# Two groups of SBUF-to-SBUF transfers of the attention layers, issued from ScalarE's queue instead of SyncE's

## The chip, the cores and the metric

The kernel runs on one core of a Trainium2 chip. The time is the device time of one execution in microseconds (us). Five engines work from queues of their own: TensorE (PE: matmuls, with the weight loads shown apart as PEld), VectorE (DVE), ScalarE (ACT), GpSimd (POOL) and SyncE (SP), which computes nothing and issues DMA transfers. They meet through semaphores: an instruction may wait until a counter has reached a value, and counts one up when it is done; a transfer counts its semaphore up by 16 when it has landed.

## The reference, cut to what matters

A batch of 32 sequences of 256 tokens and 256 features goes through two cross-attention layers and two feed-forward layers:

```python
x = x + L0_xattn(layernorm(x), ctx, ctx)    # 16 heads of 16, LoRA projections
x = x + L0_ffn(layernorm(x))                # sqrt(real^2 + imag^2)
x = x + L1_xattn(layernorm(x), ctx, ctx)    # 16 heads of 16, rotary embedding
x = x + L1_ffn(layernorm(x))                # quantised, gelu

def attention(q, k, v):                     # per batch and head
    attn = softmax(q @ k.T / sqrt(16))
    return attn @ v                         # then the output projection Wo
```

The change concerns what stands between `attn @ v` and the output projection. The kernel computes exponentials that are not normalised, multiplies them with v extended by a column of ones, and so gets for each head 16 weighted sums and the sum of the exponentials, the denominator. The division comes afterwards.

## The kernel before, in words

Both attention layers are one function, `attention`, with `layer` 0 or 1 (L0 and L1 below). It is a software pipeline over the 32 batches: each engine runs `step(i)` with 16 slots k = 0 to 15. In slot k TensorE does two matmuls of the scores of batch i + 1 (`scores`, L480) and two of the transposed scores of batch i (`scores_T`, L498); VectorE reduces the first for the row maxima (L690) and ScalarE takes the exponential of the second (L590). Both PSUM banks (`s_bank`, `t_bank`) have two halves, used in turn, so `scores_T` of slot k waits until the exponential of slot k - 2 is done (L495, semaphore `act_p`).

All other work of a batch is hung into the slots by the table `PLACE`: `"dn": (-1, 8)` says that in step i, slot 8, the engine that has the operation does it for batch i - 1. Within a slot each engine follows the order of the code. The table is an order and not a clock: SyncE's step numbers run apart from those of the others, and only the semaphores hold them together. The operations that matter here, for batch n:

- `pe0`, `pe1` (ScalarE, L600): copy the sums of half h of the heads from PSUM (`eo`) to `osb`. `pe1` is in step n + 1, slot 1 in L0 and slot 0 in L1.
- `dn` (SyncE, L270 to L273): wait for both copies, then one transfer of the denominators from 4 partitions of `osb` into `den` (128 partitions of 32).
- `mg` (SyncE, L274 to L279): wait until `den` has landed, then four transfers, each moving 16 partitions of the second half of `osb` beside the sums of the first.
- `rd` (VectorE, L706) takes the reciprocal of `den`; `rs` and `rb` (SyncE, L283, L287) send it through memory and spread it over the partitions of `rb`; `ym` (GpSimd, L378) waits for `rb` and for the merge and multiplies; `yh` and `yl` split the product, and `o0`, `o1` (TensorE, L467) are the output projection of the batch.
- SyncE's other work of a batch: twelve transfers that stack the q and k parts (`st0`, `st1`, L258), two of the maxima (`ml0`, `ml1`, L263), the context, and in L1 two for the rotation.
- ScalarE's other work in the middle of a step: `ms0` (L595, a small copy that waits for VectorE's reduction of slot 7), `qe` and `ke` (L610, the copies of the projected q and k with bias, which wait for TensorE), and in L1 `hh` (L622). `qe` of L0 is in slot 10, `qe` of L1 in slot 6, `ms0` in slot 7 in both.
- TensorE's: `q0`, `q1`, `k0`, `k1` (L460), `v0`, `v1`, `o0`, `o1` (L467), `xT` (L522), `mT0`, `mT1` (L515) and the four `pv` groups (L566).

Of the kernel before, what the change touches and what calls it, by code (L numbers as in the profile page):

```python
# [15 lines left out]
H, HD = 16, 16  # L16
RANK = 16
DFF = 1024
P = 128
# [19 lines left out]
def after(eng, sem, value):  # L39

    if not (isinstance(value, int) and value <= 0):
        eng.wait_ge(sem, value)  # L42
# [12 lines left out]
class Core:  # L55
# [12 lines left out]
    def sems(self, prefix, names):  # L68
# [20 lines left out]
)  # L89
# [72 lines left out]
def attention(core, layer, sem, f_sem, tiles, w, x_res, stats, extent, consts, src, scratch):  # L162
# [14 lines left out]
    cT, xn, xT, hl, osb, yT, yhl, rb = tiles.cT, tiles.xn, tiles.xT, tiles.hl, tiles.osb, tiles.yT, tiles.yhl, tiles.rb  # L177
    negm, mhi, mT, less_high, den, rden = tiles.negm, tiles.mhi, tiles.mT, tiles.less_high, tiles.den, tiles.rden
# [19 lines left out]
    sem = dict(sem, **core.sems(f"L{layer}", "b_load w_load rstd ones_set bvx ones0 pe_bo bo whl_q whl_k whl_v whl_o"  # L198
                                + (" rot prod sum" if rope else " lora lora_w less v_set eo_set pick high_c"
                                   " x_load0 x_load1 x_load2 x_load3 x_load4 ident")))  # L200
# [3 lines left out]
    def on(n):  # L204
        return lo <= n < hi

    def due(op, i, k):

        ahead, slot = place[op]
        return [i + ahead] if slot == k and on(i + ahead) else []  # L210
# [36 lines left out]
    def sync_program(sp):  # L247
        def all_ones():
            sp.wait_ge(sem["ones_set"], 1)
            for buf in kst:  # L250
                for u in range(2):
                    sp.dma_start(buf[64 * u + ROWS:64 * u + ROWS + 2, :, :, :].bitcast(F32), ones).then_inc(sem["ones0"], 16)

        def stack(n, h):
            u = n % 2 ^ h
            for dst, parts in ((kst[n % 2], (0, 0, 1)), (qst[n % 2], (2, 3, 2))):
                for c, part in enumerate(parts):
                    sp.dma_start(dst[64 * u + c:64 * u + ROWS:3, :, :, :].bitcast(F32), hl[h::2, part, :, :].bitcast(F32)).then_inc(sem[f"stack{h}"], 16)  # L258

        def maxima(n, h):  # L260
            u = n % 2 ^ h
            sp.wait_ge(sem["dve_mT"], 2 * n + h + 1)
            sp.dma_start(qst[n % 2][64 * u + ROWS:64 * u + ROWS + 2, :, :, :].bitcast(F32), mT[h][:, :].bitcast(F32)).then_inc(sem[f"m_load{h}"], 16)  # L263

        def step(i):
            for k in range(16):
                for h in range(2):
                    for n in due(f"ml{h}", i, k):
                        maxima(n, h)
                for n in due("dn", i, k):  # L270
                    sp.wait_ge(sem["act_eo"], 2 * n + 2)
                    after(sp, sem["dve_rd"], n)
                    sp.dma_start(den[:, :], osb[n % 2][HD:P:32, :, :, :]).then_inc(sem["den_load"], 16)  # L273
                for n in due("mg", i, k):  # L274
                    sp.wait_ge(sem["den_load"], 16 * (n + 1))
                    after(sp, sem["merge"], 64 * n)
                    for g in range(4):
                        sp.dma_start(osb[n % 2][32 * g + HD:32 * (g + 1), 0, :, :],
                                     osb[n % 2][32 * g:32 * g + HD, 1, :, :]).then_inc(sem["merge"], 16)  # L279
                for n in due("rs", i, k):  # L280
                    sp.wait_ge(sem["dve_rd"], n + 1)
                    after(sp, sem["r_load"], 16 * n)
                    sp.dma_start(r_dram.rearrange("(p n) -> p n", p=P), rden[:, :]).then_inc(sem["r_store"], 16)  # L283
                for n in due("rb", i, k):
                    sp.wait_ge(sem["r_store"], 16 * (n + 1))
                    after(sp, sem["pool_y"], n)
                    sp.dma_start(rb[:, :, :], r_dram.rearrange("(h a n) -> h a n", h=8, a=1).to_broadcast([8, HD, KT * S])).then_inc(sem["r_load"], 16)  # L287
                for h in range(2):
                    for n in due(f"st{h}", i, k):
                        sp.wait_ge(sem["pool_low"], n + 1)  # L290
                        after(sp, sem["pe_t"], 16 * (n - 2) + 8 * h + 8)
                        after(sp, sem[f"stack{h}"], 96 * n)
                        if rope and n <= lo + 1:
                            sp.wait_ge(f_sem["pe_mm"], B)
                            sp.wait_ge(f_sem["dve_x"], B)
                        stack(n, h)
                        if n == lo and h == 0:
                            all_ones()
                for n in due("ctx", i, k):
                    if rope:  # L300
                        after(sp, sem["pe_v"], max(n - 1, lo))
                        after(sp, sem["pe_k"], max(n - 1, lo))
                        after(sp, sem["ctx_load"], 16 * n)
                        sp.dma_start(cT[n % 2][:, :, :, :].bitcast(F32), c_dram[n - lo]).then_inc(sem["ctx_load"], 16)
                    else:
                        after(sp, sem["pool_c"], n - 1)
                        after(sp, sem["ctx_load"], 16 * n)
                        sp.dma_start(ctx_in[n % 2], src["ctxT"][n - lo]).then_inc(sem["ctx_load"], 16)
                if not rope:
                    for n in due("cs", i, k):  # L310
                        sp.wait_ge(sem["pool_c"], n + 1)
                        sp.dma_start(c_dram[n - lo], cT[0][:, :, :, :].bitcast(F32)).then_inc(sem["c_store"], 16)
                else:
                    for n in due("rot", i, k):
                        sp.wait_ge(sem["act_k"], n + 1)
                        sp.wait_ge(sem["act_q"], n + 1)
                        after(sp, sem["sum"], n - lo)
                        for h in range(2):
                            sp.dma_start(kqr[64 * h:64 * (h + 1), :, :, :], kq[64 * (1 - h):64 * (2 - h), :, :, :]).then_inc(sem["rot"], 16)

        return step
# [260 lines left out]
    def scalar_program(act):  # L582
        def step(i):
            for k in range(16):
# [11 lines left out]
                for h in range(2):  # L596
                    for n in due(f"pe{h}", i, k):
                        act.wait_ge(sem["pe_pv"], 4 * n + 2 * h + 2)
                        after(act, sem["pool_y"], n - 1)
                        act.activation(osb[n % 2][:, h, :, :], eo[:, :, :], ACT.Copy).then_inc(sem["act_eo"], 1)  # L600
                for n in due("xTh", i, k):
                    act.wait_ge(sem["pe_xT"], n + 1)
                    after(act, sem["pe_q"], n)
                    act.activation(xT[:, 0, :, :], bank["xT"][:, :, :], ACT.Copy).then_inc(sem["act_xT"], 1)
# [905 lines left out]
```

## Time and profile before

| | |
|---|---|
| median of 3 runs | 1902.04 us (1901.72 to 1903.93) |
| profiled execution | 1900.1 us, its span from first to last instruction 1898.3 us |
| TensorE clock granted, mean | 0.921 of full speed |
| PE busy | 1634.1 us (86%) |
| DVE, ACT, POOL busy | 1323.1, 1231.2, 848.8 us |
| all transfers, issued by SyncE | 281.34 MB, mean 148 GB/s |

The stages in order of time: a start of about 100 us, L0 to about 640 us, the first feed-forward with the first batches' preparation for L1 to about 830 us, L1 to about 1520 us, and the second feed-forward. The page gives the busy time of each engine and, in 40 slices of the span, its share in tenths with the clock that TensorE was granted. Issuing a transfer does not count as busy time; it is shown under SPq.

### The profile page before, as it was taken

Reading aid. Unit: us, or ns where it says so; the run is one execution under the profiler, and the core shown is the slowest. Engines: PE = TensorE matmul, PEld = TensorE weight load, DVE = VectorE, ACT = ScalarE, POOL = GpSimd, SP = SyncE. Lnnn points to the kernel's source line nnn. Section 1 sums busy time; section 2 is a strip of 40 time slices with the busy share of each in tenths; the row PEclk is TensorE's granted clock in tenths of the full one; section 3 lists DMA queues with packets and bytes.
Section 4 is the critical chain, followed back from the end, with each engine's and each line's share of the span. In section 5 each row is a group of like instructions: output and inputs, shape, how many; then the busy total and the mean of one; then the engine's idle time right before and its main releaser. Section 6 shows DMA issues by size and latency. Waiting matters only on the chain. (4 is left out here: it accounts for less than half of the span.)

```text
span 1898.3 us, 38948 instructions
## 1 busy us (share of the span) xinstructions
PE 1634.1 (86%) x13992; PEld 1236.5 (65%) x13992; DVE 1323.1 (70%) x2567; ACT 1231.2 (65%) x2194; POOL 848.8 (45%) x670
## 2 busy tenths in 40 slices
PE   5699999999999889778988888988989838894987
PEld 4567777777776477566666666666666536663977
DVE  5767777777777778645666767677766457776976
ACT  1267777777777678636666666666666528885875
POOL 3235555555454231145665566656665122222432
PEclk9699999999999899959899999899998759997999
DMA  8366766766776310066666666676666115557785
GB/s 249 87 142 161 151 167 161 149 165 159 155 162 152 85 50 23 17 123 141 146 140 144 144 147 147 140 150 148 152 137 138 41 39 207 213 221 270 253 274 180
DMA packets 152485, 281.34 MB, mean 148 GB/s; under 512 B 39904, under 2 KB 66144, under 8 KB 144096
## 3 DMA queue, kind: packets, MB, share of 16 engines
q1 hardware_dynamic: 152304, 278.96, 57.6%
q8 instruction: 110, 1.80, 0.5%
q14 instruction: 71, 0.58, 0.1%
HBM read 89.99 MB, written 59.77 MB: 79 GB/s over the span
## 5 line engine op out<-in xcount | busy, mean ns | idle before, releaser
L690 DVE TENSOR_REDUCE L_negm<-L_s_bank 128x2 f32<-128x512 f32 x1024 | 661.6, 682 | 364.3 <-PE L_s_bank L480 363.3
L590 ACT ACTIVATE L_prob<-L_t_bank 128x512 f32<-128x512 f32 x1024 | 573.8, 597 | 316.3 <-PE L_t_bank L498 307.6
L480 PE MATMUL L_s_bank<-L_kst,L_qst 48*128 48x256 f32 x2048 | 441.1, 327 | 60.3 <-DVE L_negm L690 45.1
L498 PE MATMUL L_t_bank<-L_qst,L_kst 50*128 50x256 f32 x2048 | 434.3, 324 | 21.2 <-ACT L_prob L590 16.4
L480 PEld LDWEIGHTS L_s_bank<-L_kst,L_qst 48*128 48x128 f32 x2048 | 301.8, 195 | 214.8 <-DVE L_negm L690 118.6
L498 PEld LDWEIGHTS L_t_bank<-L_qst,L_kst 50*128 50x128 f32 x2048 | 298.4, 194 | 35.0 <-ACT L_prob L590 24.0
L566 PE MATMUL L_eo<-L_prob,L_vext 128*17 128x256 f32 x4096 | 271.8, 397 | 3.4 <-ACT L_prob L590 3.3
L409 POOL TENSOR_TENSOR L_hl<-L_kq,L_hl 128x1024 fp32r<-128x1024 f32 x64 | 152.1, 2376 | 64.5 <-ACT L_hl L622 61.8
L1280 PE MATMUL G_acc<-G_w_out,G_hhl 128*128 128x256 f32 x1024 | 132.9, 290 | 44.8 <-DVE G_hhl L1249 44.8
L566 PEld LDWEIGHTS L_eo<-L_prob,L_vext 128*17 128x17 f32 x4096 | 103.2, 100 | 101.3 <-issue 15.6
L1280 PEld LDWEIGHTS G_acc<-G_w_out,G_hhl 128*128 128x128 f32 x1024 | 127.4, 195 | 50.6 <-issue 27.5
L610 ACT ACTIVATE L_kq<-L_misc,L_bqk 128x256 f32<-128x256 f32 x256 | 107.4, 474 | 74.6 <-PE L_misc L460 55.6
L362 POOL TENSOR_TENSOR L_kqr<-L_kqr,L_cs 128x1024 f32<-128x1024 f32 x32 | 75.9, 2373 | 161.8 <-DMA L_kqr<-L_kq 161.8
L460 PE MATMUL L_misc<-L_xT,L_wq 128*128 128x256 f32 x768 | 140.5, 326 | 2.5 <-DVE L_xT L702 1.6
L1017 PE MATMUL G_hb<-G_xT,G_w_in 128*128 128x512 f32 x512 | 127.4, 402 | 11.9 <-DVE G_xT L1127 11.2
L378 POOL TENSOR_TENSOR L_yT<-L_osb,L_rb 128x512 f32<-128x512 f32 x64 | 82.3, 1286 | 120.4 <-DMA L_rb<-r_scratch 120.2
L460 PE MATMUL L_misc<-L_cT,L_wk 128*128 128x256 f32 x768 | 119.5, 312 | 11.9 <-POOL L_cT L392 4.9
L412 POOL TENSOR_TENSOR L_yhl<-L_yT,L_yhl 128x512 fp32r<-128x512 f32 x64 | 82.6, 1290 | 102.6 <-ACT L_yhl L626 102.2
L460 PEld LDWEIGHTS L_misc<-L_xT,L_wq 128*128 128x128 f32 x768 | 114.4, 217 | 17.3 <-issue 4.3
L460 PEld LDWEIGHTS L_misc<-L_cT,L_wk 128*128 128x128 f32 x768 | 111.6, 219 | 18.1 <-issue 13.3
L1017 PEld LDWEIGHTS G_hb<-G_xT,G_w_in 128*128 128x128 f32 x512 | 94.9, 190 | 38.0 <-ACT G_hid L1059 14.2
L467 PE MATMUL L_misc<-L_wv,L_cT 128*128 128x256 f32 x768 | 119.0, 299 | 0.0
(161 smaller groups left out, 2608.6 us busy)
## 6 DMA issues: line engine op xcount, KB each, us to landing
L_kst<-L_hl SPq DMA_DIRECT2D x384, 128.0 KB, 3.4
L_qst<-L_hl SPq DMA_DIRECT2D x384, 128.0 KB, 4.1
hidden_scratch<-G_hid SPq DMA_DIRECT2D x32, 1024.0 KB, 3.9
G_hid<-hidden_scratch SPq DMA_DIRECT2D x32, 1024.0 KB, 7.4
c_scratch<-L_cT SPq DMA_DIRECT2D x32, 512.0 KB, 4.9
L_rb<-r_scratch SPq DMA_DIRECT2D x64, 256.0 KB
L_cT<-c_scratch SPq DMA_DIRECT2D x32, 512.0 KB, 3.6
L_kqr<-L_kq SPq DMA_DIRECT2D x64, 256.0 KB, 4.3
```

The costliest lines, as they stand in the source:

```text
L409: pool.tensor_tensor(KQ_LOW, kq[:, :, :, :], KQ_HIGH.bitcast(F32), ALU.subtract).then_inc(sem["pool_low"], 1)
L412: pool.tensor_tensor(yhl[:, 1, :, :], yT[:, :, :], yhl[:, 0, :, :].bitcast(F32), ALU.subtract).then_inc(sem["pool_yl"], 1)
L460: mm = pe.matmul(bank[x][:, f, :], whl[x][:, cw, k, P * f:P * (f + 1)], act[:, ca, k, :], start=j == 0, stop=j == 5)
L467: mm = pe.matmul(bank[x][:, t, :], act[:, ca, k, P * t:P * (t + 1)], whl[x][:, cw, k, :], start=j == 0 and x != "o", stop=j == 5)
L480: mm = pe.matmul(s_bank[k % 2][:, t, :], qst[n % 2][rows, j, t, P * qt:P * (qt + 1)], kst[n % 2][rows, j, t, :], start=True, stop=True)
L498: mm = pe.matmul(t_bank[k % 2][:, t, :], kst[n % 2][rows, j, t, P * kt:P * (kt + 1)], qst[n % 2][rows, j, t, :], start=True, stop=True)
L566: mm = pe.matmul(eo[SLOT * j:SLOT * j + VS, t, :], vext[n % 3][:, kt, VS * head:VS * (head + 1)], prob[h][:, kt, j, t, :], start=kt == 0, ...
L590: act.activation(prob[h][:, kt, j, :, :], t_bank[k % 2][:, :, :], ACT.Exp, scale=HD ** -0.5).then_inc(sem["act_p"], 1)
L610: ins = act.activation(kq[:, c, f, :], bank[x][:, f, :], ACT.Identity, bias=bqk[:, 1 - c, f:f + 1])
L690: dve.tensor_reduce(negm[:, h, 0, :].rearrange("p (j t q) -> p j t q", j=HJ, t=KT)[:, j, :, qt], s_bank[k % 2][:, :, :], AX.X, ALU.max, ne ...
L1017: ins = pe.matmul(hb[f % 4][:, :], w_in[:, k, P * f:P * (f + 1)], xT[q][:, c, k, :], start=j == 0, stop=j == len(group) - 1)
L1280: ins = pe.matmul(acc[i % 2][t][:, 0:D], hhl[m % 2][:, c, j, P * t:P * (t + 1)], w_out[:, f, :], start=f == 0 and c == 0, stop=f == FT - 1 ...
```

## The change

In both layers `dn` and `mg` leave SyncE's program and enter ScalarE's, behind `pe` and ahead of `xTh` in the order of a slot. They come to stand in step n + 1: `dn` in slot 3 and `mg` in slot 7 in L0, `dn` in slot 2 and `mg` in slot 6 in L1. The waits stay the same, and now ScalarE does them. Nothing else moves.

```diff
-     "pv11": (0, 15), "pe1": (-1, 1), "dn": (-1, 8), "mg": (-2, 4), "rd": (-1, 12), "rs": (-2, 2),
+     "pv11": (0, 15), "pe1": (-1, 1), "dn": (-1, 3), "mg": (-1, 7), "rd": (-1, 12), "rs": (-2, 2),
...
-     "pv10": (0, 15), "pv11": (0, 15), "pe1": (-1, 0), "dn": (-2, 9), "mg": (-3, 5), "rd": (-1, 7),
+     "pv10": (0, 15), "pv11": (0, 15), "pe1": (-1, 0), "dn": (-1, 2), "mg": (-1, 6), "rd": (-1, 7),
...
-                for n in due("dn", i, k):                      # in SyncE's step
-                    sp.wait_ge(sem["act_eo"], 2 * n + 2)
...
+                for n in due("dn", i, k):                      # in ScalarE's step
+                    act.wait_ge(sem["act_eo"], 2 * n + 2)
+                    after(act, sem["dve_rd"], n)
+                    act.dma_start(den[:, :], osb[n % 2][HD:P:32, :, :, :]).then_inc(sem["den_load"], 16)
+                for n in due("mg", i, k):
+                    act.wait_ge(sem["den_load"], 16 * (n + 1))
+                    after(act, sem["merge"], 64 * n)
+                    for g in range(4):
+                        act.dma_start(osb[n % 2][32 * g + HD:32 * (g + 1), 0, :, :],
+                                     osb[n % 2][32 * g:32 * g + HD, 1, :, :]).then_inc(sem["merge"], 16)
```

## Rows read from the trace of the kernel before

**Rows 1.** The page: busy time by engine, and TensorE's granted clock in 40 slices.
```profile
PE 1634.1 (86%) x13992; PEld 1236.5 (65%) x13992; DVE 1323.1 (70%) x2567; ACT 1231.2 (65%) x2194; POOL 848.8 (45%) x670
...
PEclk9699999999999899959899999899998759997999
```

**Rows 2.** Windows: busy time by engine, granted clock, DMA share, GB/s; L0, then L1.
```profile
100.00:640.00 540.00, 519.37 (x5501) 378.16 (x5498) 404.98 (x798) 382.58 (x778) 274.19 (x257) 1.00 0.68 156
880.00:1430.00 550.00, 491.24 (x4715) 357.73 (x4714) 374.26 (x739) 359.60 (x723) 336.65 (x207) 0.93 0.67 145
```

**Rows 3.** Windows of single steps: one of L0, two neighbours of L1.
```profile
1119.71:1139.34 19.63, 17.75 (x188) 12.93 (x184) 14.62 (x30) 13.88 (x28) 10.55 (x8) 1.00 0.70 152
1139.34:1161.45 22.11, 19.73 (x188) 14.54 (x184) 14.61 (x30) 13.99 (x28) 14.35 (x9) 0.92 0.63 141
...
392.67:410.57 17.90, 17.41 (x188) 12.82 (x184) 13.59 (x28) 12.76 (x26) 9.54 (x9) 1.00 0.70 159
```

**Rows 4.** Waits over the whole run: who waited for whom, total us, times, longest.
```profile
PEld L_s_bank L480 <- DMA L_qst<-L_hl: 14.6, 8, 11.1
...
PE L_t_bank L498 <- ACT L_prob L590: 16.4, 22, 2.4
...
PE L_s_bank L480 <- DMA L_qst<-L_hl: 11.1, 3, 10.7
```

**Rows 5.** Lines L278 and L273: issue time in ns (min/median/max), and to landing.
```profile
L278 SPq DMA_DIRECT2D L_osb<-L_osb x256: 555/589/1777, 124.6 to 1522.9; - x128
...
DMA to landing us min/median/max: 1.9/2.8/4.3
...
L273 SPq DMA_DIRECT2D L_den<-L_osb x64: 585/628/652, 108.8 to 1516.5; - x64
```

**Rows 6.** Timeline of SyncE's queue in L0: start us, length us, line, transfer, count.
```profile
410.36 3.64 SPq L278 DMA_DIRECT2D L_osb<-L_osb  x4
...
417.17 0.54 SPq L308 DMA_DIRECT2D L_kqr<-in_ctxT  x1
...
419.29 1.90 SPq L258 DMA_DIRECT2D L_kst<-L_hl  x3
```

**Rows 7.** Timeline of ScalarE in L0, slots 2 to 9 of the step begun at 410.58.
```profile
412.29 1.09 ACT L590 ACTIVATE L_prob<-L_t_bank 128x512 f32<-128x512 f32 x2
413.87 1.09 ACT L590 ACTIVATE L_prob<-L_t_bank 128x512 f32<-128x512 f32 x2 [0.49 <-PE L_t_bank L498]
415.55 1.09 ACT L590 ACTIVATE L_prob<-L_t_bank 128x512 f32<-128x512 f32 x2 [0.59 <-PE L_t_bank L498]
416.83 0.22 ACT L595 ACTIVATE L_negm<-L_negm 128x16 f32<-128x16 f32 x1 [0.20 <-DVE L_negm L690]
417.24 1.09 ACT L590 ACTIVATE L_prob<-L_t_bank 128x512 f32<-128x512 f32 x2 [0.19 <-PE L_t_bank L498]
```

**Rows 8.** Timeline of TensorE, same step: its first matmul of `scores_T` of slot 10.
```profile
417.95 0.38 PE L498 MATMUL L_t_bank<-L_qst,L_kst 50*128 50x256 f32 x1
```

**Rows 9.** Timeline of ScalarE in L1: slot 6, `qe`, slot 7.
```profile
1124.90 0.60 ACT L590 ACTIVATE L_prob<-L_t_bank 128x512 f32<-128x512 f32 x1 [0.22 <-PE L_t_bank L498]
1126.25 0.84 ACT L610 ACTIVATE L_kq<-L_misc,L_bqk 128x256 f32<-128x256 f32 x2 [0.76 <-POOL L_hl L409]
1126.98 0.60 ACT L590 ACTIVATE L_prob<-L_t_bank 128x512 f32<-128x512 f32 x1
```

**Rows 10.** Timeline of TensorE, same step: its first matmul of `scores_T` of slot 9.
```profile
1127.95 0.28 PE L498 MATMUL L_t_bank<-L_qst,L_kst 50*128 50x256 f32 x1
```

**Rows 11.** Timeline of ScalarE early in L1: a wait inside its queue.
```profile
863.12 1.06 ACT L622 ACTIVATE L_hl<-L_kq 128x1024 fp32r<-128x1024 f32 x1 [1.22 <-DMA L_qst<-L_hl]
```

**Rows 12.** Timeline of TensorE at the same place.
```profile
864.72 0.38 PE L498 MATMUL L_t_bank<-L_qst,L_kst 50*128 50x256 f32 x1 [1.73 <-ACT L_prob L590]
```

**Rows 13.** Windows around it: the stretch with the wait and the one behind it.
```profile
862.50:865.90 3.40, 1.58 (x12) 1.04 (x11) 1.50 (x4) 2.63 (x4) 1.93 (x2) 1.00 0.20 67
865.90:869.30 3.40, 3.40 (x18) 3.40 (x17) 0.80 (x2) 1.43 (x4) 1.81 (x3) 0.50 0.29 82
```

More of the change, by code:

```diff
@@ L269, in step @@
                         maxima(n, h)
-                for n in due("dn", i, k):
-                    sp.wait_ge(sem["act_eo"], 2 * n + 2)
[L272 to L279, printed above, removed]
                 for n in due("rs", i, k):
```

## The prediction, made before the changed kernel was run

> **What bounds the kernel now.** I read the page first: PE is busy 86% of the span, every other engine 70% or less, and the clock row shows dips to 9, 8 or 7 tenths in the second half [rows 1]. The average hides two stages with different limits, so I took windows next. In L0, PE is busy 519.37 of 540 us at clock 1.00; in L1 491.24 of 550 us at 0.93 [rows 2]. A single step of L0 takes 17.90 us with 17.41 us of PE; a step of L1 takes 19.63 us at clock 1.00 and 22.11 us where the clock was 0.92 [rows 3]. So L0 is bound by TensorE with 0.5 us to spare in each step: whatever holds TensorE up there is added to the time and is not made good later. L1 has some 2 us of gaps in a step, and pays for them again through the clock. ScalarE is busy 12.76 of 17.90 us in L0 [rows 3]; on the average it has room. The waits say that SyncE's transfers hardly hold TensorE up: 11.1 us of matmuls (10.7 of them once) and 14.6 us of weight loads waited for the stacks in the whole run, and 16.4 us of matmuls waited for exponentials [rows 4].
>
> **What is removed.** SyncE loses five issues a batch: four merges at a median of 0.589 us and one of the denominators at 0.628 us [rows 5], about 3.0 us of each step. What was behind them in its queue can start earlier. Since TensorE waits so little for SyncE's transfers, I value this at nothing; the most it could return is all of the 11.1 us [rows 4]. The least is minus some us, should an earlier stack collide with other traffic; the queue's order is unchanged, so I take zero. The few batches at the end of each layer, where the merge is on the chain, may win or lose about 1 us each; zero too.
>
> **What is added.** The trace has no transfer that ScalarE issues, so its price has to be bounded. The nearest row is the same instruction on SyncE: 0.589 us for a merge, one behind the other, in which time that queue does nothing else (three issues in 1.90 us, 0.63 us each with the step to the next; once four in 3.64 us) [rows 5, 6]. The lower bound is zero, if ScalarE's queue could go on to the next activation while a transfer is being issued; the upper is the 3.64 us for four. I take 0.63 us per issue, which is the usual row, and assume that nothing behind an issue starts before it is through, as on SyncE.
>
> The Trainium skill, page "DMA: Bandwidth & Descriptors", section "Issuing engines are not separate DMA queues", says that issuing from several engines only saves the sequencer's issue time, which it calls usually small beside the transfer. The proportion agrees (0.589 us against 2.8 us to landing), and by that rule the change would be worth SyncE's 3.0 us a step and cost little. The rule does not ask who pays the issue time, which is the point here.
>
> *`dn`.* In L0 it stands behind the exponential of slot 3, which begins about 412.8, the second of the pair at 412.29; the exponential of slot 4 begins at 413.87 after 0.49 us of waiting for PE [rows 7]. One issue of 0.63 us ends by 413.5 and costs nothing; if it must first wait until the exponential is finished, it costs 0.1 to 0.2 us. In L1 slot 2 has a similar gap. I take zero. Its wait is for ScalarE's own copy two slots earlier, which is done.
>
> *`mg` in L0.* The wait for `den`: issued at 412.8, landed some 2.8 us later at the median and 4.3 at the longest of the merges [rows 5], so by 415.6 to 417.1, and `mg` comes up at 416.83, behind `ms0`. It mostly finds `den` landed. Then four issues of 0.63 us, 2.5 us, from 416.85 to 419.4. The exponential of slot 8, which began at 417.24 [rows 7], begins at about 419.4, so 2.2 us late, and ends at 420.0. Behind it in ScalarE's queue are slot 9, slot 10 and `qe`; TensorE's `scores_T` of slot 10 needs the result of slot 8, which was done at 417.83 and used at 417.95 [rows 7, 8]. That leaves 0.12 us of cover: TensorE stands still for 2.1 us more, in every step with exponentials behind a finished batch, 31 of them. 31 x 2.1 = 65 us.
>
> *`mg` in L1.* It stands behind the exponential of slot 6 and ahead of `qe`. Slot 6 begins at 1124.90, the issues run to 1127.45, `qe` began at 1126.25 [rows 9]: 1.2 us late, and so is slot 7, which ends at 1128.8 instead of 1127.58. TensorE has 18 matmuls of projections at this place and asks for slot 7 only at 1127.95 [rows 10]: 0.9 us late. Where `qe` was later anyway (the slow steps) it is less. I take 0.7 us x 31 = 22 us.
>
> *The clock.* In L1 there is a small model of this change. ScalarE waited 1.22 us for a transfer inside its queue [rows 11], TensorE stood still for 1.73 us waiting for the exponential [rows 12], and behind the stretch with this gap (PE busy 1.58 of 3.40 us) the granted clock was 0.50, the level of 1.2 GHz, for the next one, though PE was busy in all of it [rows 13]. L0 has had no such gap and no fall (clock 1.00 over 540 us). A gap of 2.1 us in each step will bring such falls into it. Price of one: half of about 3.4 us of TensorE's work, 1.7 us, where PE is dense; in L1 the step with clock 0.92 took 22.11 - 19.63 = 2.48 us more [rows 3]. I take a fall in three steps of four in L0: 31 x 0.75 x 1.75 = 41 us (bounds 0 and 31 x 2.48 = 77). In L1, 0.93 over 550 us is already 77 us at half clock, a fall in nearly every step; the longer gap adds perhaps one in four steps, 31 x 0.25 x 2.48 = 19 us.
>
> **The sum.** 65 + 22 + 41 + 19 = 147 us on the profiled execution's 1900.1 us (span 1898.3 us): 2047 us. The median of the runs is 1.9 us above it: 2049 us.
>
> **The rivals.**
>
> *The clock does not fall in L0.* For it: the falls of L1 follow several gaps a step and not one. Against it: rows 12 and 13. 1902 + 65 + 22, with or without the 19: 1989 to 2008 us.
>
> *ScalarE's queue hides part of the issues,* because activations already sent on keep the engine busy, or an issue costs it half. With 0.3 us per issue slot 8 is 0.9 us late in L0 and L1 pays nothing: 31 x 0.8 = 25 us, with a few falls of the clock 1925 to 1960 us. For it: the issue is no engine time; against it: SyncE, which has nothing but its queue, does none faster than 0.555 us, and activations wait for TensorE, so none are sent ahead.
>
> *Both queues hold each other up.* If the generation of descriptors is one resource, an issue of ScalarE waits for the one that SyncE is in. In L0 SyncE issues little between 416.8 and 419.3 (0.54 us at 417.17), then three in 1.90 us [rows 6]; in L1 it may be more. An issue would then take up to 1.2 us and four of them 5 us: some 2 us more in each of 62 steps at the worst, 1902 + 147 + 124 = 2173 us; I place this case at 2110 to 2175.
> The Trainium skill says so: page "Perfetto Trace Analysis", section "DMA Instruction — HWDGE (DVE, Sync)", has the unit locked for exclusive use by one sequencer at a time. No trace of before can show it, as only SyncE issues.
>
> *The change does nothing measurable:* issues wholly hidden in ScalarE's 5.1 us of free time a step (17.90 - 12.76), 1902 us. Against it: the free time lies elsewhere, in pieces below 0.6 us around slots 3 to 8 [rows 7].
>
> *Faster.* SyncE, free of 3.0 us a step, sends the stacks earlier, and TensorE's waits for them go: 11.1 us and the clock's share, 1888 to 1892 us. This decides only if an issue costs ScalarE less than about 0.2 us, so that four fit between the start of `ms0` and slot 8 (0.4 us) and behind its 0.12 us of cover.
>
> **How the numbers follow.** Forecast 0.50 (its own range 2005 to 2100); clock holds in L0 0.17; partly hidden 0.13; both queues hold each other up 0.10; nothing 0.05; faster 0.05. A change below 0.2% cannot be told from none here. So faster 0.05, within 0.2% 0.05, slower 0.90. The range takes in the case with the steady clock and the upper part of the hidden one, and ends inside the case of contention: 1935 to 2130.
>
> **What would show it.** The profile after should have five issues a batch under ACTq at about 0.6 us; the exponential of slot 8 in L0 about 2.5 us behind `ms0`; a wait of PE L498 for ACT L590 grown from 16.4 us to 80 or 90 us; L0's steps at 20 us where the clock is full and near 22 us where it fell; a clock below 1.00 in L0. The forecast is wrong if the exponentials of slots 8 and 9 begin where they did (issues are hidden), if L0's clock stays 1.00, if the issues last 1 us and more, or if ScalarE is seen waiting for `den` at `mg`.

## The result, and the profile after

The changed kernel takes 2047.4 us in the median (2043.01 to 2051.95) against 1901.88 us for the kernel before in the same session: slower, ratio 1.0771 (95% interval 1.0735 to 1.0806). Its profiled execution has a span of 2041.2 us, 142.9 us more than before. Of the kernel `e_o0` below, one execution of four took 2373.57 us at a mean clock of 0.58, where the other three took 1884 to 1889 us; it is left out of its time. The page after, the lines that answer to [rows 1]:

```profile
PE 1700.2 (83%) x13992; PEld 1269.4 (62%) x13992; DVE 1331.9 (65%) x2567; ACT 1235.9 (61%) x2194; POOL 847.9 (42%) x670
...
PEclk9588888888888877996899999999999767997999
```

No engine got more work, apart from TensorE, whose 66 us more are the same matmuls at a lower clock. The new low clock is in the first half, in L0.

Windows over the same steps of both kernels say where the time went. The columns are those of [rows 2]; the first line is L0 from its first exponential to that of step 31, the second L1 from step 34 to 63. Before:

```profile
84.00:639.14 555.14, 533.89 (x5585) 388.98 (x5585) 414.15 (x814) 390.37 (x794) 278.64 (x261) 0.99 0.68 155
858.86:1477.03 618.17, 552.60 (x5287) 400.75 (x5283) 419.06 (x826) 401.58 (x805) 371.64 (x225) 0.93 0.66 144
```

After:

```profile
84.17:767.58 683.41, 610.97 (x5585) 435.79 (x5585) 417.24 (x814) 393.42 (x793) 277.88 (x261) 0.87 0.53 126
992.64:1616.25 623.61, 537.82 (x5287) 385.32 (x5283) 425.57 (x826) 403.13 (x805) 371.60 (x225) 0.96 0.68 143
```

L0 has grown by 128.3 us, 4.1 us in each of 31 steps. L1 has grown by 5.4 us only, and its clock has risen from 0.93 to 0.96. The other 9.2 us lie between the layers and at the end.

The same place in a step of L0, first ScalarE (the columns are start, length, line; "x4" are four issues in a row; "idle" stands in brackets with its releaser), as in [rows 7]:

```profile
310.87 1.09 ACT L580 ACTIVATE L_prob<-L_t_bank 128x512 f32<-128x512 f32 x2 [0.58 <-PE L_t_bank L488]
312.16 0.21 ACT L585 ACTIVATE L_negm<-L_negm 128x16 f32<-128x16 f32 x1 [0.20 <-DVE L_negm L690]
312.22 2.45 ACTq L599 DMA_DIRECT2D L_osb<-L_osb  x4
314.77 1.78 ACT L580 ACTIVATE L_prob<-L_t_bank 128x512 f32<-128x512 f32 x3 [2.40 <-DMA L_osb<-L_osb]
```

then TensorE, as in [rows 8]:

```profile
312.66 0.28 PE L505 MATMUL L_misc<-ident,L_negm 128*32 128x128 f32 x1
313.27 0.38 PE L470 MATMUL L_s_bank<-L_kst,L_qst 48*128 48x256 f32 x1 [0.33 <-DVE L_negm L690]
315.43 0.38 PE L488 MATMUL L_t_bank<-L_qst,L_kst 50*128 50x256 f32 x1 [1.77 <-ACT L_prob L580]
```

Before, the first `scores` behind the same transpose (L505 here, L515 there) had this wait and no other:

```profile
417.95 0.38 PE L480 MATMUL L_s_bank<-L_kst,L_qst 48*128 48x256 f32 x1 [0.33 <-DVE L_negm L690]
```

The windows of 3.40 us before the gap, with it, and behind it:

```profile
309.30:312.70 3.40, 3.40 (x34) 2.77 (x30) 2.62 (x5) 2.29 (x5) 3.31 (x2) 1.00 0.78 223
312.80:316.20 3.40, 1.30 (x13) 0.73 (x16) 1.89 (x5) 1.33 (x3) 1.87 (x2) 1.00 0.48 149
316.20:319.60 3.40, 3.40 (x29) 2.14 (x18) 1.63 (x3) 2.17 (x5) 0.00 (x0) 0.50 0.89 180
```

The four issues begin 0.06 us behind the start of `ms0` and hold ScalarE's queue for 2.45 us. The exponential of slot 8 begins 2.61 us behind `ms0`; before it was 0.41 us [rows 7]: 2.2 us late. TensorE stands still for 0.33 and 1.77 us where it had waited 0.33 us, and behind the stretch in which it was busy 1.30 of 3.40 us the clock is 0.50 though it is busy all the time. This is the pattern of [rows 12, 13], now in every step. Over the whole run the wait that was 16.4 us [rows 4] has become

```profile
PE L_t_bank L488 <- ACT L_prob L580: 98.3, 72, 2.9
```

What `dn` does is seen in the same queue. The issue runs from 418.12 to 418.72. The exponential of slot 2 runs beside its start and that of slot 3, which stands ahead of it in the queue, beside the rest; slot 4 then waits 0.49 us for TensorE, as before:

```profile
417.83 0.60 ACT L580 ACTIVATE L_prob<-L_t_bank 128x512 f32<-128x512 f32 x1
418.12 0.60 ACTq L594 DMA_DIRECT2D L_den<-L_osb  x1
418.32 0.59 ACT L580 ACTIVATE L_prob<-L_t_bank 128x512 f32<-128x512 f32 x1
419.40 1.09 ACT L580 ACTIVATE L_prob<-L_t_bank 128x512 f32<-128x512 f32 x2 [0.49 <-PE L_t_bank L488]
```

The price of an issue on ScalarE, all 256 merges (min/median/max in ns), beside 555/589/1777 on SyncE [rows 5]:

```profile
L599 ACTq DMA_DIRECT2D L_osb<-L_osb x256: 514/611/1762, 112.1 to 1665.1; - x128
...
  ACT L_prob L580: 81.4, 33
  ACT L_kq L610: 68.0, 28
...
DMA to landing us min/median/max: 1.9/2.4/4.2
```

The two lines in the middle name who waited for these issues: 81.4 us of exponentials, most in L0, and 68.0 us of `qe`, in L1.

### The profile page after: what moved, and what is told of

It is laid out like the page before. It is cut to its first block and busy times, and to the rows that moved or that the text cites. A ratio compares the mean times of both kernels' runs of the same rounds, so it can differ in the third digit from the quotient of the medians.

```text
span 2041.2 us, 38948 instructions
## 1 busy us (share of the span) xinstructions
PE 1700.2 (83%) x13992; PEld 1269.4 (62%) x13992; DVE 1331.9 (65%) x2567; ACT 1235.9 (61%) x2194; POOL 847.9 (42%) x670
## 5 line engine op out<-in xcount | busy, mean ns | idle before, releaser
L488 PE MATMUL L_t_bank<-L_qst,L_kst 50*128 50x256 f32 x2048 | 458.0, 336 | 99.8 <-ACT L_prob L580 98.3
L470 PE MATMUL L_s_bank<-L_kst,L_qst 48*128 48x256 f32 x2048 | 466.7, 338 | 58.9 <-DVE L_negm L690 44.5
L470 PEld LDWEIGHTS L_s_bank<-L_kst,L_qst 48*128 48x128 f32 x2048 | 317.0, 204 | 226.2 <-DVE L_negm L690 119.6
L488 PEld LDWEIGHTS L_t_bank<-L_qst,L_kst 50*128 50x128 f32 x2048 | 313.2, 204 | 122.1 <-ACT L_prob L580 114.9
L556 PE MATMUL L_eo<-L_prob,L_vext 128*17 128x256 f32 x4096 | 297.0, 425 | 3.3 <-ACT L_prob L580 3.3
L457 PE MATMUL L_misc<-L_wv,L_cT 128*128 128x256 f32 x768 | 132.3, 322 | 0.0
L450 PE MATMUL L_misc<-L_cT,L_wk 128*128 128x256 f32 x768 | 109.3, 294 | 11.2 <-DVE L_xT L702 4.2
L457 PEld LDWEIGHTS L_misc<-L_wv,L_cT 128*128 128x128 f32 x768 | 115.2, 222 | 5.0 <-issue 0.7
L457 PE MATMUL L_misc<-L_wo,L_yhl 128*128 128x256 f32 x768 | 118.0, 292 | 0.0
```

The source lines that it names most:

```text
L450: mm = pe.matmul(bank[x][:, f, :], whl[x][:, cw, k, P * f:P * (f + 1)], act[:, ca, k, :], start=j == 0, stop=j == 5)
L457: mm = pe.matmul(bank[x][:, t, :], act[:, ca, k, P * t:P * (t + 1)], whl[x][:, cw, k, :], start=j == 0 and x != "o", stop=j == 5)
L470: mm = pe.matmul(s_bank[k % 2][:, t, :], qst[n % 2][rows, j, t, P * qt:P * (qt + 1)], kst[n % 2][rows, j, t, :], start=True, stop=True)
L488: mm = pe.matmul(t_bank[k % 2][:, t, :], kst[n % 2][rows, j, t, P * kt:P * (kt + 1)], qst[n % 2][rows, j, t, :], start=True, stop=True)
L556: mm = pe.matmul(eo[SLOT * j:SLOT * j + VS, t, :], vext[n % 3][:, kt, VS * head:VS * (head + 1)], prob[h][:, kt, j, t, :], start=kt == 0, ...
```

## The experiments

Times of all runs, with the two layers' steps from windows over the same steps as above. "Low" is the time at half clock, worked out as (1 - granted clock) x length / 0.5; since the clock is shown to two digits, it can be some 7 us off. The trace's own record of the clock, in which the falls below are counted, gives for L0 13.7 us before (one piece at the start of the layer and no fall after it), 177.4 us after and 23.3 us in `e_fill`, and for L1 88.7 us before, 44.4 us after, 81.9 us in `e_fill15`, 54.6 us in `e_o0` and 41.0 us in `e_o0_fill4`. The layers' times are those of one profiled execution each; that of `e_fill15` was 9.6 us below its median.

| kernel | median us | ratio to before (95%) | L0, us (clock) | L1, us (clock) | low L0, L1 |
|---|---|---|---|---|---|
| before | 1901 to 1903 | | 555.1 (0.99) | 618.2 (0.93) | 11, 87 |
| after | 2047.4 | 1.0771 (1.0735 to 1.0806) | 683.4 (0.87) | 623.6 (0.96) | 178, 50 |
| e_l0_only | 2041.87 | 1.0716 (1.0674 to 1.0758) | 688.7 (0.87) | 621.3 (0.93) | 179, 87 |
| e_l1_only | 1908.54 | 1.0033 (1.001 to 1.0056) | 557.8 (0.98) | 619.8 (0.96) | 22, 50 |
| e_dn_only | 1902.98 | 1.0001 (0.9979 to 1.0024) | 555.4 (0.99) | 621.1 (0.93) | 11, 87 |
| e_busy | 2042.53 | 1.0734 (1.0695 to 1.0773) | 683.1 (0.88) | 623.8 (0.96) | 164, 50 |
| e_fill | 1984.97 | 1.0418 (1.039 to 1.0445) | 625.8 (0.98) | 627.8 (0.95) | 25, 63 |
| e_two | 1933.62 | 1.0156 (1.0112 to 1.0201) | 589.8 (0.97) | 617.6 (0.94) | 35, 74 |
| e_slot15 | 1926.03 | 1.0137 (1.0106 to 1.0169) | 567.5 (0.98) | 621.6 (0.93) | 23, 87 |
| e_l1_len | 1914.47 | 1.0073 (1.0055 to 1.0092) | 555.4 (0.99) | 629.3 (0.96) | 11, 50 |
| e_fill15 | 1904.07 | 1.0005 (0.9982 to 1.0029) | 554.8 (0.99) | 612.2 (0.93) | 11, 86 |
| e_o0 | 1885.53 | 0.9912 (0.9887 to 0.9936) | 556.0 (0.99) | 598.1 (0.95) | 11, 60 |
| e_o0_hh | 1908.83 | 1.0039 (1.0015 to 1.0063) | 555.1 (0.99) | 626.8 (0.95) | 11, 63 |
| e_o0_fill4 | 1890.41 | 0.9942 (0.9917 to 0.9967) | 557.1 (0.98) | 606.9 (0.97) | 22, 36 |

**Which layer.** Both functions are kept, and the layer decides which is used (here and below the entries of the table alone, with the layer and the engine noted beside them):

```diff
-    "dn": (-1, 8), "mg": (-2, 4)        # L0, SyncE
+    "dn": (-1, 3), "mg": (-1, 7)        # L0, ScalarE:  if not rope: ...
...
     "dn": (-2, 9), "mg": (-3, 5)        # L1, SyncE:    if rope: ...
```

> The change made in layer 0 alone; layer 1 keeps its transfers on SyncE. In the trace of the changed kernel the 31 steps of L0 took 683 us instead of 555, those of L1 624 instead of 618. Theory (the cost is TensorE standing still behind ScalarE's four issues in L0, and the clock falling with it): nearly the whole loss is here, +125 to +140 us, 2028 to 2042 us. Rival (my own split on record: L1 costs 41 us): +106 us, about 2008 us.

Measured 2041.87 us. The mirror image, the change in L1 alone:

> The change made in layer 1 alone. Theory: a step without a fall of the clock gets 1.4 us longer (19.6 to 21.1 us), but there are fewer falls; net +5 to +15 us, 1907 to 1917 us, clock in L1 above 0.93. Rival (each longer gap brings more falls, as on record): +41 us, about 1943 us. If the smaller number of falls was chance of how the steps lay, this run comes out between.

Measured 1908.54 us. L0 is 140 us of the loss and L1 is 6 us, and the two add up to the whole; the split on record (106 and 41) was wrong. The theory held in both.

**Which transfer.** `dn` goes to ScalarE in its new places, `mg` stays with SyncE:

```diff
+    "dn": (-1, 3), "mg": (-2, 4)        # L0
+    "dn": (-1, 2), "mg": (-3, 5)        # L1
```

> Only the transfer of the denominators goes to ScalarE (its new places); the four merges stay on SyncE in their old places. Theory: one issue of 0.6 us fits into ScalarE's idle time at slot 3 (L0) and 2 (L1); L0's steps stay at 17.9 us, total 1900 +- 5 us. Rival (any issue on ScalarE costs, by its length or because both queues want the same generator): 0.3 us or more a step, 1912 us and up.

Measured 1902.98 us, no difference. One issue of 0.6 us per step on ScalarE, placed where it waits for TensorE, costs nothing.

**Issues or just the queue.** No transfer is moved; ScalarE is given extra work at the place of the merges:

```diff
+                for n in due("bz", i, k):                  # (-1, 7) in L0, (-1, 6) in L1
+                    for m in range(5):
+                        after(act, sem["busy"], 5 * n + m - 1)
+                        act.activation(tiles.busy[:, (5 * n + m) % 2, :], eps[:, 0:1].to_broadcast([P, 512]), ACT.Copy).then_inc(sem["busy"], 1)
```

> No transfer is moved. At the place of the merges (slot 7 of L0, slot 6 of L1) ScalarE does five extra activations of 128x512 into a tile that nobody reads, some 2.5 us in all. Theory (what costs is only how long ScalarE's queue is held): L0's steps go to 22 us as with the merges, total 2025 to 2060 us. Rival (the cost comes from transfers issued from a second queue, by contention or by late landing): the total stays nearer to 1902 us than to 2047 us.

Measured 2042.53 us, L0 683.1 us against 683.4 us after. The same step in its timeline:

```profile
311.52 0.22 ACT L596 ACTIVATE L_negm<-L_negm 128x16 f32<-128x16 f32 x1 [0.20 <-DVE L_negm L695]
311.65 2.69 ACT L605 ACTIVATE L_busy<-eps 128x512 bf16<-128x512 f32 x5
314.24 1.76 ACT L591 ACTIVATE L_prob<-L_t_bank 128x512 f32<-128x512 f32 x3
```

ScalarE is held for 2.6 us by work instead of issues, with every transfer where it was, and the loss is all there. So neither contention of two queues nor where or when the merges land is needed for the loss, and nothing is left for them to explain. It also prices SyncE's relief: this run has SyncE as loaded as before and comes out no slower than the change (5 us faster), so the relief of 3 us a step is worth nothing.

Contention can be looked for in the trace of the changed kernel as well. In both steps shown, SyncE issues while ScalarE's four merges (312.22 to 314.67, and 1299.06 to 1301.56 in L1, below) are being issued:

```profile
313.80 0.65 SPq L263 DMA_DIRECT2D L_qst<-L_mT  x1
...
1300.05 1.88 SPq L258 DMA_DIRECT2D L_kst<-L_hl  x3
```

The four merges take 2.45 and 2.50 us all the same and the three stacks 0.63 us each, as in [rows 6]. Of the 256 merges, 147 run beside an issue of SyncE, with medians of 0.611 us in L0 and 0.612 us in L1; the 109 others have 0.611 us in L0 and 0.530 us in L1. In `e_slot15` below 235 of the 256 run beside one, at 0.611 and 0.612 us.

**Standing still or the clock.** The changed kernel, with matmuls that fill the gap:

```diff
+                if not rope and k == 9 and on(i) and on(i - 1):
+                    pe.wait_ge(sem["act_eo"], 2 * i)
+                    for _ in range(18):
+                        pe.matmul(eo[0:VS, 0, :], whl["q"][:, 0, 0, 0:VS], whl["q"][:, 0, 0, :], start=True, stop=True)
```

> The changed kernel with 18 extra matmuls (17 columns of weights, 256 moving, into a PSUM bank that is free then) in slot 9 of L0, just where TensorE stands still for some 2 us behind ScalarE's issues. They change no result and add 31 x 18 matmuls of about 0.12 us, which fit into the gap. Theory (about half of L0's loss is the clock): the granted clock of L0 goes back to 1.00, its steps from 22.1 to 20.0 or 20.3 us, total 1980 to 1992 us. Rival (the clock's fall is not caused by this gap, or costs nothing because PE waits anyway): L0's steps stay at 22 us or get longer, 2045 us and up.

Measured 1984.97 us, 62 us less than after, by giving TensorE 558 matmuls more to do. The window of L0, and the filled gap of a typical step in the timeline:

```profile
84.51:710.27 625.76, 605.57 (x6125) 443.90 (x6125) 416.93 (x814) 390.29 (x794) 278.48 (x261) 0.98 0.58 137
```

```profile
274.18 0.28 PE L505 MATMUL L_misc<-ident,L_negm 128*32 128x128 f32 x1
274.22 2.30 PE L510 MATMUL L_eo<-L_wq 128*17 128x256 f32 x18
276.45 0.38 PE L470 MATMUL L_s_bank<-L_kst,L_qst 48*128 48x256 f32 x1
276.94 0.38 PE L488 MATMUL L_t_bank<-L_qst,L_kst 50*128 50x256 f32 x1
```

The step behind it shows the opposite case. Its four merges took 3.87 us, so behind the 18 matmuls TensorE still stood still for 1.49 us, and there the clock fell, one of only two falls in this layer.

L0's loss of 128.3 us thereby splits: 625.76 - 555.14 = 70.6 us are the standing still (2.28 us a step), 683.41 - 625.76 = 57.7 us the clock. The split is good to some 5 us. A typical step of `e_fill` takes 19.96 us against 17.91 us before, 2.05 us more; the rest of its 70.6 us comes from 8 blocks of merges that took 2.7 to 3.9 us, and the changed kernel had only 2 such blocks. By that its standing still is nearer to 65 us and its clock nearer to 63 us. The steps agree: in the changed kernel a step with 3.4 us at half clock takes 21.49 us and one with 6.8 us takes 22.86 us, 1.5 and 2.9 us more than 19.96 us.

**The dose.** Two of the four merges on ScalarE, two on SyncE in the old place:

```diff
+                    for g in (0, 1):        # in ScalarE's step
+                    for g in (2, 3):        # in SyncE's step
```

> The denominators and two of the four merges on ScalarE, the other two merges on SyncE in their old place. ScalarE's queue is held 1.25 us instead of 2.5 us. Theory: slot 8 of L0 comes 0.9 us late, of which 0.8 us reach TensorE; such a gap brings few falls of the clock, so the step is 18.7 us and L1 gains or loses little: +25 to +40 us, 1927 to 1942 us. Rival (proportional, half of the loss): about 1975 us. Rival (a threshold elsewhere): unchanged 1902 us.

Measured 1933.62 us, a ratio of 1.0156: half of the issues cost a fifth of the time. A step without a fall takes 18.68 us, 0.77 us more than before, and TensorE's gap there is 0.82 us (0.33 and 0.49 us). It brought 7 falls of the clock in 31 steps of L0, where the whole block brought 30; the proportional rival is excluded, for both the standing still and the falls are less than half.

**The place.** All four merges on ScalarE, behind the copies of k and v of slot 15:

```diff
+    "dn": (-1, 3), "mg": (-1, 15)       # L0
+    "dn": (-1, 2), "mg": (-1, 15)       # L1
```

> Denominators on ScalarE as in the change; the four merges on ScalarE too, but in slot 15 of step n + 1, behind the copies of k and v, where ScalarE waits 1.6 us (L0) and 3.5 us (L1) for TensorE anyway. Theory: L1 pays nothing, L0 2.5 - 1.6 = 0.9 us a step at most, less what TensorE has in hand at slot 0: 1902 to 1935 us. Rival (transfers on ScalarE's queue cost wherever they stand): 2000 us and up. Rival (relieving SyncE of 3.0 us a step is worth something): below 1897 us.

Measured 1926.03 us. The same four issues cost 12.4 us in L0 there and 3.4 us in L1 (the profiled span is 21.7 us longer; the rest lies between the layers). In L0 the slot's 1.6 us of idle time do not hold 2.5 us and the remainder shows, 0.4 us a step, with one fall of the clock, at the layer's end. Of SyncE's relief nothing is seen here either.

**Why L1 lost so little.** The mechanism is there as in L0. ScalarE, then TensorE, as in [rows 9, 10]:

```profile
1298.74 0.60 ACT L580 ACTIVATE L_prob<-L_t_bank 128x512 f32<-128x512 f32 x1 [0.22 <-PE L_t_bank L488]
1299.06 2.50 ACTq L599 DMA_DIRECT2D L_osb<-L_osb  x4
1301.67 0.84 ACT L610 ACTIVATE L_kq<-L_misc,L_bqk 128x256 f32<-128x256 f32 x2 [2.33 <-DMA L_osb<-L_osb]
1302.40 0.60 ACT L580 ACTIVATE L_prob<-L_t_bank 128x512 f32<-128x512 f32 x1
```

```profile
1303.05 0.38 PE L488 MATMUL L_t_bank<-L_qst,L_kst 50*128 50x256 f32 x1 [1.09 <-ACT L_prob L580]
```

ScalarE waited here for `den`, which the prediction took as landed: in 20 of the 29 steps the first merge is issued within 0.05 us of `den`'s landing, which comes 3.8 us (median) after its issue, against 2.3 us in L0. A step at full clock takes 21.06 us instead of 19.63 us [rows 3]:

```profile
1293.59:1314.65 21.06, 18.11 (x188) 13.12 (x184) 14.88 (x30) 13.98 (x29) 13.46 (x9) 1.00 0.72 147
```

That is 1.4 us a step, 41 us over 29 steps; but another wait has gone. Before, ScalarE's `hh` waited for GpSimd's rotated q and k; in a stretch of 550 us of L1 it did so for 14.5 us before and 1.5 us after (first line before, second after):

```profile
ACT L_hl L622 <- POOL L_kq L406: 14.5, 13, 2.7
```

```profile
ACT L_hl L622 <- POOL L_kq L396: 1.5, 2, 1.2
```

The test is a longer step without a gap and without any transfer moved, 12 extra matmuls in slot 9 of L1:

```diff
+                if rope and k == 9 and on(i) and on(i - 1):
+                    pe.wait_ge(sem["act_eo"], 2 * i)
+                    for _ in range(12):
+                        pe.matmul(eo[0:VS, 0, :], whl["q"][:, 0, 0, 0:VS], whl["q"][:, 0, 0, :], start=True, stop=True)
```

> The kernel before with 12 extra matmuls in slot 9 of L1, which change no result: TensorE is busy some 1.4 us longer in each step and nobody stands still. Question: why does the change cost L1 so little, 5 us of 619, when a step without a fall got 1.4 us longer? Theory (a longer step gives GpSimd time to finish the rotated q and k, so that ScalarE no longer waits for it in hh, and the gap behind that wait goes and with it part of the falls): the same here, L622's wait for POOL falls from 14.5 us to 3 us or less, falls in L1 from 20 to about 10, steps of 21.0 to 21.4 us, total 1895 to 1910 us. Rival (SyncE, relieved of its issues, sent the stacks earlier): SyncE is not relieved here, so the wait and the falls stay and the total is 1925 to 1945 us.

Measured 1914.47 us, 5 us beyond the upper end of what was expected. What was foreseen of the mechanism is there: in the same stretch the wait of `hh` for GpSimd is not in the list at all, the clock of L1 is 0.96 and the falls are 11 instead of 20, as after (11 too). The relief of SyncE is not needed for it. A reading that fits both runs, and is not shown step by step: GpSimd's chain through the rotation could not follow steps of 19.6 us for long; waits for it and falls of the clock came now and then and made the mean 21.3 us, and steps of 21.1 us hardly run into them. The new wait took the place of the old ones. That the vanished waits are also the cause of the fewer falls is not shown apart from the longer step.

**Filling the gaps of L1.** Ten matmuls like those of the filled gap above, in slot 15 of L1 of the kernel before, ahead of `o0`:

```diff
+                if rope and k == 15 and on(i):
+                    pe.wait_ge(sem["act_eo"], 2 * i + 1)
+                    for _ in range(10):
+                        pe.matmul(eo[0:VS, 0, :], whl["q"][:, 0, 0, 0:VS], whl["q"][:, 0, 0, :], start=True, stop=True)
```

> The kernel before with 10 extra matmuls in slot 15 of L1, in the gap of 1.25 us in which TensorE waits for VectorE ahead of o0; they change no result. Theory (that gap is what brings most falls of the clock in L1): low time in L1 from 89 us to 30 us or less, steps from 21.3 to 20.0 us, total 1860 to 1870 us. Rival (the falls come as well from the gap behind hh in slot 5): low time 50 to 70 us, total 1880 to 1895 us.

Measured 1904.07 us, no difference, and hardly less low time (81.9 us against 88.7 us). The theory fell, and the rival's figure was too good as well. The largest gap of L1 is not what brings its clock down: of the 20 falls before, 4 came right behind it and 15 behind slots 0 to 6. Filled, it is followed by none, but there are 17 falls, 16 of them behind slots 0 to 6 (slots by ScalarE's exponentials just ahead of the fall).

**A version that beats both.** Real work in place of the gap, one entry of the table:

```diff
-     ... "yl": (-2, 8), "o0": (-2, 15), "o1": (-3, 5),
+     ... "yl": (-2, 8), "o0": (-3, 0), "o1": (-3, 5),
```

> The kernel before with one operation of L1 moved: the first half of the output projection (o0) from slot 15 to slot 0 of the next step, so that the second weighted sums (pv10, pv11) come ahead of it. It waited 1.25 us in each of 26 steps of L1 for VectorE. Theory (gaps of TensorE cost twice, once themselves and once through the clock): the gap shrinks to 0.5 us or less, the clock of L1 rises from 0.93 to 0.98 or more, its steps go from 21.3 to 19.0 or 19.5 us: 1840 to 1865 us. Rival (the falls in L1 come from its other gaps): 0.7 us a step, 1880 us, clock near 0.93.

Measured 1885.53 us, ratio 0.9912 (0.9887 to 0.9936), the fastest of all (1887 us in the two texts below). It lies outside both ranges, nearer to the rival: L1 is 20.1 us shorter, its clock 0.95 and not 0.98. The low time fell by 34 us, from 88.7 to 54.6 us, so part of the 20 us may be the clock; how much is the gap itself is not shown. Two attempts to go on from there:

```diff
-     "rb3": (2, 0), "hh": (2, 3), "hl": (2, 0),
+     "rb3": (2, 0), "hh": (2, 5), "hl": (2, 0),
```

> The kernel before with o0 of L1 in slot 0 of the next step, as in the run that took 1887 us, and hh of L1 (ScalarE's rounding of the rotated q and k) moved from slot 3 to slot 5, where TensorE has o1 and 18 projections ahead of it. Theory (what is left of L1's gaps is the one at slot 5, where scores_T waits for an exponential that stands behind hh): that gap of 0.5 to 1.2 us goes, few falls stay, steps of 19.0 to 19.6 us, total 1840 to 1860 us. Rival (GpSimd's chain through the rotation is then the bound, and moves its wait to another place): 1875 to 1890 us.

Measured 1908.83 us, slower than before. `hh` two slots later makes GpSimd's `hl` later and with it `qe`, which waits for it: in the stretch 900 to 1450 us

```profile
ACT L_kq L610 <- POOL L_hl L409: 51.4, 25, 2.1
```

against 10.3 us in 13 waits before and 13.6 us in 16 in `e_o0`. The rival's mechanism is right and its price was too low.

```diff
+                if rope and k == 4 and on(i) and on(i - 1):
+                    pe.wait_ge(sem["act_eo"], 2 * i)
+                    for _ in range(5): ...      # the same matmul as above
```

> The kernel before with o0 of L1 in slot 0 of the next step, and 5 extra matmuls in slot 4 of L1, ahead of the place where scores_T waits for the exponential behind hh; they change no result and take some 0.6 us. Theory (what brings the clock down in L1 is the thinly filled stretch of slots 1 to 5 with that gap at its end, as the run with slot 15 filled suggests, where 17 falls stayed): low time of L1 from 55 us to 30 us or less, total 1865 to 1880 us against 1887. Rival (the matmuls only take time, where ScalarE is in time): 1890 to 1905 us, low time unchanged.

Measured 1890.41 us (ratio 0.9942, 0.9917 to 0.9967), not distinguishable from the run without the fill. Low time in L1 fell from 54.6 to 41.0 us and L1 got 8.8 us longer, so the matmuls took more than that gave back. The theory fell; the rival's time was right, though it had the low time unchanged.

## Why the prediction was right, and where it was not

The time was forecast at 2049 us and is 2047.4 us; the mechanism is the one named. That the figures lie so close is partly luck: the two terms of L0 came out 22 us above the forecast and 9 us appeared outside the layers, where nothing was forecast, while the two terms of L1 came out 36 us below.

- *What bounds the kernel:* right. L0 had nothing to make a hold-up good with, and all of it came through.
- *Removal:* valued at nothing, and `e_busy` shows that it is nothing, to within some 5 us.
- *Price of an issue:* 0.63 us with the step to the next, from SyncE's row; on ScalarE 0.611 us at the median, four in 2.45 to 2.50 us where undisturbed.
- *`dn`:* zero, as said (`e_dn_only`). It is even beside running exponentials.
- *`mg` in L0:* 2.1 us a step and 65 us forecast; 2.05 us in a typical step, and 70.6 us over the layer with the single long blocks of `e_fill` (nearer to 65 us in the changed kernel, which had fewer).
- *The wait of L498 for L590:* 80 or 90 us forecast, 98.3 us measured.
- *The clock in L0:* 41 us forecast, 57.7 us measured. The step that was mis-sized is "a fall in three steps of four": there was one in practically every step (30 in 31, about half of them of double length), low time 177 us. The price of a single one was nearly right, 1.75 us in the sum and 1.5 us measured.
- *`mg` in L1:* 22 us forecast. At full clock a step became 1.4 us longer, not 0.7. In the step shown the first issue waited until 0.3 us behind slot 6, for `den`, and TensorE stood still for 1.09 us. The prediction had reckoned with 2.8 us to the landing, from the merges' row; in L1 it was 3.8 us. A wait for `den` at `mg` was one of its own signs of being wrong, and in L1 that sign came true.
- *The clock in L1:* this step failed. It said that the longer gap adds a fall in one step of four, 19 us; the falls went from 20 to 11 and the low time from 88.7 to 44.4 us. Its starting point was off too: 20 falls in 29 steps, touching 17 of them, are not "a fall in nearly every step". Both L1 terms together were 41 us and came out at 5.4 us. What was missed, by the reading above, is that L1 was already held by a second chain (GpSimd's), whose wait the new one replaced; the row that says so (L622 waiting for L406, 14.5 us) stands in none of the prediction's rows and has no term in its sum.
- *The rivals:* the steady clock is excluded (0.87 in L0), as are partly hidden issues (slot 8 is 2.2 us late), no effect and a faster kernel. Both queues holding each other up does not show: a merge takes 611 ns at the median on ScalarE against 589 on SyncE, issues of the two queues run at the same time and are longer by 0.08 us at most in the median, and `e_busy` loses the same time without any issue on ScalarE. The rule of the Trainium skill that the unit is locked for exclusive use ("Perfetto Trace Analysis", section "DMA Instruction — HWDGE (DVE, Sync)") would make one sequencer wait for the other. The trace does not show how long the unit is locked within an issue; it shows that 147 merges beside an issue of SyncE lasted 0.61 us at the median, so a lock for the length of an issue is excluded. The rule of the Trainium skill in "DMA: Bandwidth & Descriptors", section "Issuing engines are not separate DMA queues", is right in what it says (only issue time is saved) and that saving was worth nothing to a kernel that did not wait for SyncE; what counted was on whose queue the time is spent.

Open is what in slots 0 to 6 of L1 brings the clock down; the fills at slots 15 and 4 did not settle it, and this was not followed further.

## What to carry to other kernels

Issuing a transfer cost the issuing queue its 0.6 us on SyncE and on ScalarE alike, and a compute engine's free share (ScalarE had 5.1 us in 17.9) says nothing about a block of 2.5 us: look at the longest piece of idle time at that place, and at what TensorE needs from the next instruction in that queue. One issue in a piece of idle time was free, four in a row ahead of an operand of the bounding engine cost 4 us a step. In L0 a gap of some 2 us in TensorE's stream was paid nearly twice, once as itself and once as low clock behind it, and in L1, with a second chain close behind, the new wait took the place of an old one: price it from the rows of that chain, not from the gap.

## What the runs showed of the hardware that was not expected

- An issue on ScalarE's queue does not stop the activation that has been sent on: at 418.12 to 418.72 it ran beside two exponentials. It stops the one that stands behind it: after the four issues that end at 314.67 the next exponential begins at 314.77.
- Two queues can issue at the same time: 147 of the 256 merges on ScalarE ran beside an issue of SyncE, with a median of 0.61 us against 0.61 us (L0) and 0.53 us (L1) without one.
- A kernel may gain time from more work for TensorE: 558 matmuls without use took 62 us off the changed kernel, since the granted clock of L0 went from 0.87 to 0.98.
- The clock does not fall behind the largest gap by rule. In L1 a gap of 1.25 us in each step could be filled with hardly a change in the low time (82 us against 89), whereas in L0 the filling of 2.1 us removed nearly all (23 against 177). In `e_two` the same gap of 0.82 us was followed by a fall in 7 of 31 steps and not in the others.
